# Reading the moving operand of a hi/lo-split matmul chain from the last column to the first

## The reference

```python
x = x + L0(x, cond)   # x @ W_base.T + b, plus a low-rank term of 8 experts mixed by cond
x = x + L1(x, cond)   # the two best experts of 8, weighted, and a shared one; each is
                      # (gelu(x @ gate) * (x @ up)) @ down, with a hidden width of 512
x = x + L2(x, cond)   # the best expert: (silu(x @ up + b) * (x @ gate + b)) @ down + b, width 256
x = x + L3(x, cond)   # x @ (sum over experts of cond * weight * mask).T + bias
```

## Time and profile before

| what | us |
|---|---|
| median of 3 runs (lowest to highest) | 74.33 (74.02 to 75.19) |
| the profiled execution's own time | 73.86 |
| its span, first to last instruction | 71.9 |
| TensorE busy, matmuls | 65.8 |
| TensorE busy, weight loads (beside the matmuls) | 52.9 |
| ScalarE busy | 48.9 |
| VectorE busy | 47.8 |
| GpSimd busy | 38.2 |

### The profile page before, as it was taken

How to read it: one execution, slowest core, us unless ns; L and a number is a source line. 1 busy time by engine, 2 the same in 40 slices (tenths; PEclk the granted TensorE clock), 3 DMA queues, 4 the chain that set the end, 5 groups by cost and what they waited for, 6 DMA issues and landing times.

```text
span 71.9 us, 1094 instructions
## 1 busy us (share of the span) xinstructions
PE 65.8 (92%) x303; PEld 52.9 (74%) x303; DVE 47.8 (67%) x93; ACT 48.9 (68%) x94; POOL 38.2 (53%) x48
## 2 busy tenths in 40 slices
PE   4946799999999999999999999999999999999850
PEld 4933588888888888888888888888888877685720
DVE  0072908996667777666666777669698779959930
ACT  5166849588766666787666667887968969456520
POOL 5120148419999999987999996645555000000000
PEclk9999999999999999999999999999999999999999
DMA  0699999999700000000000000000000000000034
GB/s 0 138 256 351 325 359 364 419 424 411 279 38 0 0 14 0 0 5 0 0 0 0 0 0 0 0 0 9 0 0 0 0 0 0 0 0 0 0 146 146
DMA packets 2740, 6.62 MB, mean 92 GB/s; under 512 B 432, under 2 KB 1456, under 8 KB 2736
## 3 DMA queue, kind: packets, MB, share of 16 engines
q1 hardware_dynamic: 2448, 6.18, 23.5%
q10 hardware_dynamic: 288, 0.39, 1.5%
HBM read 6.04 MB, written 0.52 MB: 91 GB/s over the span
## 4 chain that ended last, share of the span: by engine, by line
PE 85%; DMA 5%; SPq 2%; DVE 2%; issue 1%; ACT 1%
PE acc L418 9%; PE gp L414 9%; PE up L415 9%; PE up L418 9%; PE up L414 9%; PE acc L415 9%; PE gp L415 9%; PE gp L418 9%; PE acc L414 9%; DMA raw_shared<-shared 5%; PE gp L525 2%; PE acc L429 1%; PE gp L530 1%; DVE wlo L564 1%; ACT whi L322 1%
## 5 line engine op out<-in xcount | busy, mean ns | idle before, releaser
L350 ACT ACTIVATE act<-gp 128x512 f32<-128x512 f32 x24 | 14.4, 599 | 11.9 <-PE gp L418 10.5
L599 DVE TENSOR_TENSOR hlo<-up,hhi 128x512 fp32r<-128x512 f32 x27 | 18.4, 682 | 0.8 <-ACT hhi L337 0.7
L271 POOL TENSOR_TENSOR wlo<-raw_skill,whi 128x384 fp32r<-128x384 f32 x16 | 16.3, 1020 | 4.8 <-ACT whi L322 4.7
L591 DVE SCALAR_TENSOR_TENSOR up<-up,gate_w,act 128x512 f32<-128x512 f32 x16 | 12.1, 758 | 9.5 <-ACT act L350 8.9
L337 ACT ACTIVATE hhi<-up 128x512 fp32r<-128x512 f32 x27 | 16.0, 594 | 2.3 <-DVE up L584 2.0
L414 PE MATMUL acc<-hhi,whi 128*128 128x512 f32 (+1 forms) x28 | 11.1, 396 | 0.0
L418 PE MATMUL acc<-hlo,whi 128*128 128x512 f32 (+1 forms) x28 | 10.9, 388 | 0.0
L414 PE MATMUL gp<-xhi,whi 128*128 128x512 f32 x27 | 10.6, 392 | 0.1
L415 PE MATMUL acc<-hhi,wlo 128*128 128x512 f32 (+1 forms) x28 | 10.7, 381 | 0.0
L414 PE MATMUL up<-xhi,whi 128*128 128x512 f32 x27 | 10.5, 389 | 0.0
L415 PE MATMUL up<-xhi,wlo 128*128 128x512 f32 x27 | 10.5, 389 | 0.0
(11 more groups left out here) (102 smaller groups left out, 93.7 us busy)
## 6 DMA issues: line engine op xcount, KB each, us to landing
raw_skill<-skill SPq DMA_DIRECT2D x4, 768.0 KB, 8.9
raw_l<-l SPq DMA_DIRECT2D x2, 386.5 KB, 9.3
raw_shared<-shared SPq DMA_DIRECT2D x4, 192.0 KB, 3.9
w3in<-l SPq DMA_DIRECT2D x1, 576.0 KB, 7.8
x<-x_t SPq DMA_DIRECT2D x2, 256.0 KB, 3.5
out_t<-res ACTq DMA_DIRECT2D x1, 256.0 KB, 2.1
params<-l SPq DMA_DIRECT2D x1, 128.0 KB, 2.5
out_t<-res ACTq DMA_DIRECT2D x1, 128.0 KB, 1.7
```

The lines of the kernel that those rows point to most:

```text
L271: pool.tensor_tensor(wlo[:, p, :], raw_piece(p), whi[:, p, :], ALU.subtract).then_inc(s_wlo, 1)
L350: sc.activation(act[:, k % 2, :], gp[k % PAIRS][:, :], ACT.Gelu_apprx_tanh).then_inc(s_act, 1)
L591: ve.scalar_tensor_tensor(out=out, in0=u, scalar=gate_w[:, b, r:r + 1], in1=a, op0=ALU.mult, op1=ALU.mult).then_inc(s_h, 1)
L599: ve.tensor_tensor(hlo[:, i, t], hidden_of(k, t), hhi[:, i, t], ALU.subtract).then_inc(s_hlo, 1)
```

## The change

A helper `along` turns a moving operand's columns round, by a step of -1 on the free axis, for the blocks 1 to 25. `gate_up` uses it on `xhi` and `xlo`, and `down` on `hhi` and `hlo`. What a turned `gate_up` leaves in `gp` and `up` lies with its columns reversed, and so do `act`, the gated product, `hhi` and `hlo` of that block. The turned `down` reads these backwards, so that `acc` is in the order of before. Outputs in PSUM are written forwards as before, and weights are read as before.

```diff
+            def along(k, v):
+                return v[:, ::-1] if 0 < k < N1 + L2_BLOCKS else v
+
             def gate_up(k, fresh_input=False):
...
-                x_h, x_l = xhi[:, layer, b, :], xlo[:, layer, b, :]
+                x_h, x_l = along(k, xhi[:, layer, b, :]), along(k, xlo[:, layer, b, :])
...
             def down(k):
                 p, i, out = piece_of(k), k % HBUFS, acc[BLOCK_BATCH[k]][:, :]
                 wait_down(k)
-                hi_passes(out, whi[:, p, 2 * P:], wlo[:, p, 2 * P:], hhi[:, i, :], is_first(k))
+                hi_passes(out, whi[:, p, 2 * P:], wlo[:, p, 2 * P:], along(k, hhi[:, i, :]), is_first(k))
                 pe.wait_ge(s_hlo, k + 1)
-                lo_pass(out, whi[:, p, 2 * P:], hlo[:, i, :], is_last(k)).then_inc(s_d, 1)
+                lo_pass(out, whi[:, p, 2 * P:], along(k, hlo[:, i, :]), is_last(k)).then_inc(s_d, 1)
```

## The result

The changed kernel takes 75.61 us in the median of 18 runs (75.15 to 76.65) against 74.45 us (73.84 to 75.20) of the kernel before in 18 runs beside it: a ratio of 1.0154, with a 95% interval of 1.0119 to 1.0188. That is 0.9 to 1.4 us slower. The change was forecast to cost nothing, and it costs a small, clear amount.

The account below looks back on a forecast made before the run. TensorE was taken as the bound, busy 53.43 of 53.56 us in the turned stretch. Profiled execution of 73.86 us plus 225 x 0 gave 73.86, forecast as a median of 74.2 us, range 73.5 to 77.3.

Parts of the forecast that it names:

- What bounds the kernel: Stretch from block 1's first matmul to after down(25): TensorE sets the pace, busy 53.43 of 53.56 us.
- The count and the untouched rest: Blocks 1 to 25: 225 matmuls turned, no instruction added or removed, ScalarE's and VectorE's work on gated products unchanged.
- The open price: What a step of -1 on the moving operand adds to each float32r matmul of 512 columns, 225 times over.
- I take the value zero: Turned matmuls cost nothing extra, since the same bytes are read and consecutive columns stay neighbours: 225 x 0.
- its own sign of being wrong: The distance between turned matmuls grows by more than 6.6 ns; 225 x 6.6 ns is 1.48 us, 2% of the time.
- the likeliest case: Turned matmuls keep the same rate: median 74.2 us, own range 73.5 to 75.1, chance 0.70.
- The rival of a fixed cost: Each turned matmul pays at its start, at most 13.3 ns more, 3.0 us in all, giving 76.9 us; chance 0.10.
- its test in the profile: Fixed cost's sign: nine matmuls of a middle block take 2.10 us or more, untouched down(0) and gate_up(26) matmuls stay 0.227 apart.
- Half rate: Rival: turned matmuls read one column in two cycles, 203 ns more each, 45.7 us in all, giving 119.6 us; chance 0.14.
- two records: Rival: turned matmuls run like plain float32 in two records, 633 ns more each, 142 us, giving 216 us; chance 0.04.
- The symmetry argument: SBUF reads of turned operands: a backward walk meets four float32 in every 16-byte line like a forward one, so +0.

## Why the prediction was wrong

**What bounds the kernel: right.** TensorE sets the time of the stretch, nothing covers it, and 225 turned matmuls passed their whole price on but for 0.11 us of the 0.51 us of waits that the prediction had found.

**The count and the untouched rest: right.** The instructions are the same, VectorE's and ScalarE's operations on a block's gated product take the same time to within 1% (`act` 598 ns in place of 599, `hlo` 681 in place of 682), and the granted clock stayed 1.00 in the stretch.

**The open price: wrong.** The step that failed is "I take the value zero", on the ground that the same bytes are read and consecutive columns are still neighbours. The term was 6.67 ns for a matmul, against bounds of 0 and 13.3 ns for a fixed cost and 203 ns for half the rate. It lies just over the 6.6 ns that the prediction named as its own sign of being wrong. The ground itself failed: with the same bytes and neighbours still side by side, the order of the read moved the distance from 226.7 to 233.3 ns. The time of 75.61 us is inside the stated range (73.5 to 77.3), which was drawn wide enough to hold a rival, but outside the likeliest case's own (73.5 to 75.1). It is also within 2% of the time before, to which the prediction gave 0.70. That was the chance of an unchanged distance, and the distance did change: that the price came to 1.5% and not to more is luck. The prediction reckoned that 2% is as fine as one can measure here; 18 runs of each kernel leave an interval of 0.7%, and the move is clear of noise where none was forecast.

**The rival of a fixed cost: nearer in size, wrong in mechanism.** It gave 76.9 us, and its test in the profile came out in one half: the block turns are 2.10 us. The other half, untouched matmuls that still lie 0.227 us apart, came out only roughly. The three of `down(0)` take 0.70 us between turned ones, where they took 0.68 before; those of `gate_up(26)` stand behind the longest wait and, after the first, lie 0.22 to 0.24 us apart, as they did before. And the price is not paid at the start of an instruction: at 256 columns the backward read is cheaper by about 2 ns, at 384 dearer by 4, at 512 by 6.7. The prediction split a matmul into 0.417 ns a column and 13.3 ns fixed from forward rows alone, and doubled the fixed part to price the change. Backwards the split is another one: some 0.449 ns a column with 3.3 ns fixed, by the line through 256 and 512 columns, which gave the widths between them to within 2 ns. As forward matmuls in mixed company lie on the same line below 512 columns, this is a description of the distances and not yet a rate of the backward read.

**Half rate and two records: excluded**, as the prediction held likely; the 303 records stayed single, and by that line a column takes 8% longer, not twice as long.

**The symmetry argument, and the page beside it.** The Trainium skill ("SBUF — State Buffer", section "SBUF: two separate sides") reckons with lines of 16 bytes, by which, as the prediction worked out, a backward walk would have cost nothing. The measured price is not nothing, and the measurement decides. What the segments show is a coarser piece: the order inside 256 bytes matters (2.09 to 2.10 us with segments of 32 columns or fewer), while turning round pieces of 256 bytes or more costs nothing (2.04 us).

**What stays open.** Why a read from the last column to the first takes longer is not shown; the runs exclude the setup of an instruction, the place of the first address as the sole cause, and the load of the weights. Nor is it shown why a forward stream loses its 226.7 ns next to shifted operands, with narrower weights, or with other widths around it. At 512 columns the cheap forward matmul looks like the special case: it needs an even stream, and in mixed company, with narrower weights or one column off it takes 230 to 237 ns on the mean. None of the theories accounts for one thing more: the distances at which streams settle, 120.0, 146.7, 173.3, 226.7 and 233.3 ns, are 18, 22, 26, 34 and 35 times 6.67 ns, while the means between them belong to streams that swing from one matmul to the next (115 to 123 ns backwards at 256 columns). So the price in this kernel is one such step, and whether a backward read of 512 columns needs all of it, or less and is held up to the next step, no run shows.

## To carry to other kernels

Where TensorE is the bound and works without a break, a few nanoseconds on each matmul show: price the operand's access order as a term of its own, with a range, even where the bytes are the same. The forward, evenly placed, full-width stream is a rate to be kept; turning whole pieces of 64 columns costs nothing here, while turning pieces of 32 columns or fewer costs 3% and a start one column off costs 4%. A cost that a row gives for one width should be measured at a second width before it is called fixed.

## What the hardware showed that was not expected

- At 256 columns a backward read was not dearer than a forward one (118 against 120.0 ns), at 512 it was (233.3 against 226.7).
- Segments read in falling order cost nothing from 64 columns up (2.04 us a block), nearly the full price at 32 (2.09 us) and all of it at 16 or fewer (2.10 us).
- Fewer columns of weights made forward matmuls of 512 columns slower: 226.7, 230 and 232 ns at 128, 64 and 32 columns of weights. At 384 columns they did not: 173.3 ns at 128 and at 32.
- Forward matmuls whose own operand was unshifted became dearer for a while behind shifted ones (a `gate_up` of 1.39 us in place of 1.36), and went back to 226.7 ns later.
